# A gated attention and lookup-table FFN kernel: new orders in each group of 512 tokens, and one ScalarE copy for both halves of a looked-up block

## The reference

```python
xn = layernorm(x)                                  # x: 8 x 1024 x 512, fp32, rows of 512
q, k_i, v_i = xn @ Wq, xn @ Wk[i], xn @ Wv[i]      # 3 heads i, 128 wide
gate = softmax(xn @ Wg)                            # 3 numbers for a token
w_i = sigmoid(decay_logits[i]) ** max(s - t - 1, 0) where s > t, else 0   # diff = s - t
blended = sum_i gate_i * ((q @ k_i.T) * w_i) @ v_i
s = blended @ Wo * out_scale
G, U, Dn = lut[gate_idx], lut[up_idx], lut[down_idx]   # 16-entry table; 1376 x 512, 1376 x 512, 512 x 1376
h = silu(xn @ G.T) * (xn @ U.T)
y = x + s * silu(h @ Dn.T)
```

## Time and profile before

| | |
|---|---|
| three executions | 1935.11, 1935.36, 1942.34 us, median 1935.36 |
| profiled execution, its own time | 1939.05 us |
| its span | 1937.2 us |
| setup / 16 groups | 0 to 139.7 / 139.7 to 1937 us |
| mean granted TensorE clock | 0.987 |
| TensorE (PE) busy | 1826.7 us, 94% |
| VectorE (DVE), GpSimd (POOL), ScalarE (ACT) busy | 66%, 53%, 41% |

### The profile page before, as it was taken

The page is one execution under the profiler, slowest core; times in us unless marked ns, Lnnn a source line. Parts: engine busy times, 40 slices in busy tenths (PEclk is TensorE's granted clock), DMA queues, the critical chain, the costliest instruction groups (busy, mean ns, idle before and its releaser), DMA issues. The chain is left out here.

```text
span 1937.2 us, 45221 instructions
## 1 busy us (share of the span) xinstructions
PE 1826.7 (94%) x15944; PEld 1421.2 (73%) x15944; DVE 1287.3 (66%) x2629; ACT 803.3 (41%) x1445; POOL 1025.4 (53%) x1041
## 2 busy tenths in 40 slices
PE   6899999999999999899999999999999999999997
PEld 2337878687886878688776878768786887878786
DVE  7867657475865857476674758657574866748574
ACT  3773444343443343343443434333443434444342
POOL 9204728274562827447281745628283573828353
PEclk9999999999999999999999999999999999999999
DMA  9966666758675675757666686856767676676653
GB/s 227 350 241 165 176 183 164 191 162 225 157 184 165 172 199 159 212 154 186 184 164 176 162 221 157 195 159 172 198 160 204 157 195 183 161 195 164 184 152 106
DMA packets 401850, 354.53 MB, mean 183 GB/s; under 512 B 221553, under 2 KB 277617, under 8 KB 401537
## 3 DMA queue, kind: packets, MB, share of 16 engines
q1 hardware_dynamic: 390608, 344.57, 65.7%
q0 software_dynamic: 11008, 6.89, 2.4%
HBM read 277.56 MB, written 35.52 MB: 162 GB/s over the span
## 5 line engine op out<-in xcount | busy, mean ns | idle before, releaser
L1846 PE MATMUL F<-xtc,ring 128*128 128x256 f16 (+1 forms) x4224 | 501.2, 273 | 1.5 <-DVE region L1498 1.5
L1846 PEld LDWEIGHTS F<-xtc,ring 128*128 128x128 f16 (+1 forms) x4224 | 416.5, 100 | 45.9 <-DVE region L1498 3.5
L1846 PE MATMUL F<-xt,ring 128*128 128x256 f16 (+1 forms) x3168 | 385.8, 273 | 47.6 <-DVE region L1486 47.6
L1885 PE MATMUL F<-ring,region 128*128 128x256 f16 x3360 | 392.2, 277 | 0.0
L1846 PEld LDWEIGHTS F<-xt,ring 128*128 128x128 f16 (+1 forms) x3168 | 307.2, 100 | 92.7 <-DVE region L1486 60.0
L1885 PEld LDWEIGHTS F<-ring,region 128*128 128x128 f16 x3360 | 333.4, 99 | 52.9
L823 POOL TENSOR_TENSOR region<-hs,region 128x1024 f16<-128x1024 f32 x80 | 175.4, 2193 | 63.2 <-ACT region L909 63.2
L839 POOL TENSOR_TENSOR x_sb<-x_sb,region 128x512 f32<-128x512 f32 x64 | 81.0, 1265 | 192.0 <-DVE region L1585 192.0
L1731 PE MATMUL B<-xt,a_hi 128*128 128x512 f16 x512 | 158.4, 392 | 22.2 <-issue 17.5
L785 POOL TENSOR_TENSOR rstd<-var,nhalf 128x4 f32<-128x4 f32 x15 | 15.3, 1019 | 280.2 <-DVE var L1174 280.2
L909 ACT ACTIVATE region<-region 128x256 f16<-128x256 f32 x192 | 94.4, 500 | 166.5 <-DVE region L1518 166.5
(11 more groups left out here) (272 smaller groups left out, 3466.3 us busy)
## 6 DMA issues: line engine op xcount, KB each, us to landing
ring<-blocks SPq DMA_DIRECT2D x546, 256.0 KB, 3.1
ring<-dblocks SPq DMA_DIRECT2D x224, 256.0 KB, 3.1
x_sb<-in_x SPq DMA_DIRECT2D x64, 256.0 KB, 3.3
out_y<-x_sb SPq DMA_DIRECT2D x64, 256.0 KB, 3.5
ring<-blocks SPq DMA_DIRECT2D x112, 128.0 KB, 2.5
ring<-dblocks SPq DMA_DIRECT2D x112, 128.0 KB, 2.7
blocks<-ring SPq DMA_DIRECT2D x35, 256.0 KB, 8.0
x_sb<-codes SPq DMA_DIRECT2D x10, 512.0 KB, 9.2
```

What stands on the lines that cost most here:

```text
L1846: ins = T_.matmul(out_, a, b, start=fresh, stop=False, skip_group_check=True)
L1885: ins = T_.matmul(bank[:, j * HV:(j + 1) * HV], a, b, start=fresh, stop=False, skip_group_check=True)
```

## The change

The setup's two copies of a unit (high, low) become one over two neighbouring PSUM banks; `wd_hi` and `wd_lo` become one tensor. In the groups: the x work of tiles 0 and 1 moves to the values and the first set; the last set gets buffers of its own for YC and ZC (YB, ZB), so that its u4 need not wait for h2 of set 4, and that h2 moves behind c22 of set 5; `h_sums_high` of a set moves behind the first_copy two sets on; low2 of set 5 goes ahead on GpSimd; scores, retrieve and others shift; a copy of one column (`warm`) opens ScalarE's group 0 of an iteration; and TensorE does the next group's queries and keys ahead of the loop's end. `vb32` moves out of `xp`.

```diff
-            n += 4
+            n += 2
...
-        SCORES = {2: 0, 12: 1, 24: 2, 34: 3}
-        RETRIEVE = {6: 0, 17: 1, 29: 2}
-        PROBS = {3: 0, 13: 1, 25: 2}
-        LOWPR = {4: 0, 14: 1, 26: 2}
-        MIX = {11: 0, 18: 1}
+        SCORES = {3: 0, 12: 1, 24: 2, 34: 3}
+        RETRIEVE = {7: 0, 17: 1, 29: 2}
+        PROBS = {4: 0, 13: 1, 25: 2}
+        LOWPR = {5: 0, 14: 1, 26: 2}
+        MIX = {11: 0, 20: 1}
         UPDATE = {9: 0, 18: 1, 30: 2}
-        ROWS1 = {16: 0, 36: 1}
-        ROWS2 = {17: 0, 38: 1}
-        BLEND = {20: 0, 41: 1}
+        ROWS1 = {16: 0, 27: 1}
+        ROWS2 = {17: 0, 27: 1}
+        BLEND = {20: 0, 30: 1}
-        XHAT = {10: 0, 12: 1}
-        XLOW = {11: 0, 13: 1}
-        XPOSE = {15: 0, 17: 1}
-        XSUM = {16: 0}
-        XSUMHI = {20: 0}
-        XSUMLO = {22: 0}
+        XHAT = {1: 0, 3: 1}
+        XPOSE = {8: 0, 10: 1}
+        XSUMHI = {3: 0}
+        XSUMLO = {5: 0}
...
+        YB = [YC] * ND + [XC[ND % 2][:, 1:2]]
+        ZB = [ZC] * ND + [SC[ND % 2][:, 1:2]]
-        vb32 = xp[:, 0, 0:HD]
+        vb32 = at["bl"][:, 0:HD]
...
@@ GpSimd, a group @@
+                if not last:
+                    x_low(0)
+                    x_low(1)
+                    x_sums(0)
                 for n in range(NPG):
...
+                low2(ND)
                 h_sums_low(ND - 1)
                 low1(ND)
-                low2(ND)
@@ ScalarE, store in the setup @@
-                        copy(held(s, op, 0), LUHI[b % 2][:, n * w:n * w + w]).then_inc(s_wst, 1)
-                        copy(held(s, op, 1), LULO[b % 2][:, n * w:n * w + w]).then_inc(s_wst, 1)
+                        copy(held(s, op, slice(0, 2)), LU[b % 2][:, :, n * w:n * w + w]).then_inc(s_wst, 1)
@@ ScalarE, a group @@
+                if g == 0:
+                    copy(warm[:, :], dlog[:, 0:1])
...
                     copy(vb_hi[:, t], vb32[:, :]).then_inc(s_vbh, 1)
+                    if t in XHAT and not last:
+                        act.wait_ge(s_dwr[ND - 1], 16)
+                        x_high(XHAT[t], gi * GT + GT + XHAT[t] + 1)
...
                     if p == 0:
                         first_copy(s)
+                        if s >= 2:
+                            h_sums_high(s - 2)
                         if s:
                             high1(s - 1)
-                    if p == 1 and s:
+                    if p == 1 and 0 < s < ND:
                         high2(s - 1)
                     if p == 4:
                         silu1(s)
+                        if s == ND:
+                            high2(s - 1)
                     if p == 5:
                         silu2(s)
-                        if s:
+                        if s == ND:
                             h_sums_high(s - 1)
@@ VectorE, the values of a group @@
                     V_.tensor_tensor(vb_lo[:, t], vb32[:, :], vb_hi[:, t], ALU.subtract).then_inc(s_vbl, 1)
+                    if t in XHAT and not last:
+                        if XHAT[t] == 0:
+                            dve.wait_ge(s_tt, (gi * 2 + 2) * NTT)
+                            dve.wait_ge(s_xlo, gi * GT + GT)
+                        xhat_tile(1 - g, gi + 1, XHAT[t])
@@ VectorE, the sets @@
                 def u4(s):
-                    if s:
-                        dve.wait_ge(s_h2, q)
-                    else:
-                        dve.wait_ge(s_yr, gi * GT + FREE)
+                    if s == 0:
+                        dve.wait_ge(s_yr, gi * GT + FREE)
+                    elif s < ND:
+                        dve.wait_ge(s_h2, q)
...
                     if p == 1:
                         u2(s)
-                        if s:
+                        if 0 < s < ND:
                             h2(s - 1)
...
                     if p == 3:
                         c22(s)
+                        if s == ND:
+                            h2(s - 1)
@@ TensorE @@
+            queries_keys(0, 0)
             with pe.Fori(0, NB - 1) as i:
-                for g in range(GPB):
-                    group(i, g, False)
-            for g in range(GPB):
-                group(NB - 1, g, g == GPB - 1)
+                group(i, 0)
+                queries_keys(i, 1)
+                group(i, 1)
+                queries_keys(i + 1, 0)
+            group(NB - 1, 0)
+            queries_keys(NB - 1, 1)
+            group(NB - 1, 1)
```

More of the change, by code:

```diff
@@ L251, in attention_ffn_kernel @@
         oscale = sb("oscale", [P, 1], F32)
+        warm = sb("warm", [P, 1], F32)
         fade_q = sb("fade_q", [P, NH], F32)
@@ L351, in landed @@
             return 16 * (b // SLOTS + (b % SLOTS >= NDIR))
-        FB = [ps("F1"), ps("F2"), ps("F3"), ps("F4")]
+        fb = ctx.enter_context(nc.psum_tensor("F", [P, 4, BANK], F32))
+        FB = [fb[:, n] for n in range(4)]
         B = [ps("B0"), ps("B1"), ps("B2"), ps("B3")]
-        LUHI = [FB[0], FB[1]]
-        LULO = [FB[2], FB[3]]
+        LUHI = [FB[0], FB[2]]
+        LULO = [FB[1], FB[3]]
+        LU = [fb[:, 0:2], fb[:, 2:4]]
         s_x = [sem("x_in0"), sem("x_in1")]
@@ L948, in store @@
                         v0 = HV if u[0] == "ends" else 0
[L949 to L952, removed]
+                        to = stage[half[0]][:, half[1]] if half else wd[:, :, v0:v0 + HV]
+                        copy(to, LU[b % 2][:, :, at0:at0 + HV]).then_inc(s_wst, 1)
                 else:
@@ L1095, in group @@
                         high_probs(PROBS[n])
-                    if n in XHAT and not last:
-                        act.wait_ge(s_dwr[ND - 1], 16)
-                        x_high(XHAT[n], gi * GT + GT + XHAT[n] + 1)
                     if n in XSUMHI and not last:
@@ L1480, in u4 @@
                     dve.wait_ge(s_u2, q + 1)
-                    if s:
+                    if s == 0:
+                        dve.wait_ge(s_yr, gi * GT + FREE)
+                    elif s < ND:
                         dve.wait_ge(s_h2, q)
-                    else:
-                        dve.wait_ge(s_yr, gi * GT + FREE)
                     dve.wait_ge(s_pp, gi * NPG + s * NP + 3)
-                    V_.tensor_tensor(YC[0:M, 0:w], pair(3, s), XC[s % 2][0:M, 0:w], ALU.add).then_inc(s_u4, 1)
+                    V_.tensor_tensor(YB[s][0:M, 0:w], pair(3, s), XC[s % 2][0:M, 0:w], ALU.add).then_inc(s_u4, 1)
                 def c22(s):
@@ L1491, in c22 @@
                     dve.wait_ge(s_pp, gi * NPG + s * NP + 4)
-                    V_.tensor_tensor(ZC[0:M, 0:w], pair(2, s), YC[0:M, 0:w], ALU.add).then_inc(s_c22, 1)
+                    if s == ND:
+                        dve.wait_ge(s_hl2, q - 1 + 2 * FREE)
+                    V_.tensor_tensor(ZB[s][0:M, 0:w], pair(2, s), YB[s][0:M, 0:w], ALU.add).then_inc(s_c22, 1)
                 def c12(s):
@@ L1517, in h2 @@
                     dve.wait_ge(s_sg2, q + 1)
-                    V_.scalar_tensor_tensor(out=SC[s % 2][0:M, 0:w], in0=YC[0:M, 0:w], scalar=f_hf[0:M, 0:1],
-                                            in1=ZC[0:M, 0:w], op0=ALU.mult, op1=ALU.mult).then_inc(s_h2, 1)
+                    V_.scalar_tensor_tensor(out=SC[s % 2][0:M, 0:w], in0=YB[s][0:M, 0:w], scalar=f_hf[0:M, 0:1],
+                                            in1=ZB[s][0:M, 0:w], op0=ALU.mult, op1=ALU.mult).then_inc(s_h2, 1)
                 for n in range(NPG):
@@ L1549, in group @@
                         low_probs(gi, LOWPR[n])
-                    if n in XHAT and not last:
-                        j = XHAT[n]
-                        if j == 0:
-                            dve.wait_ge(s_vbl, gi * GT + GT)
-                        xhat_tile(1 - g, gi + 1, j)
                 c21(ND)
@@ L1779, in retrieve, with queries_keys @@
                 ins.then_inc(s_pu, 1)
-            def group(i, g, last):
+            def queries_keys(i, g):
                 gi = i * GPB + g
@@ L1795, in group @@
                                       xh[:, k], xl[:, k]) for k in range(KC)], GRP).then_inc(s_pqk, 1)
+            def group(i, g):
+                gi = i * GPB + g
+                xh, xl = xt_hi[:, g], xt_lo[:, g]
                 for t in range(GT):
@@ L1863, in chunk @@
                         hh, hl = ht[0:M, 0, cols], ht[0:M, 1, cols]
-                        wh, wl = wd_hi[0:M, v * HV:(v + 1) * HV], wd_lo[0:M, v * HV:(v + 1) * HV]
+                        wh, wl = (wd[0:M, half, v * HV:(v + 1) * HV] for half in range(2))
                         for a, b in ((hh, wh), (hh, wl), (hl, wh)):
```

13 lines of the change are left out of this document (5 added, 8 removed).

## The result

The changed kernel took 1969.24 us (median of four runs, 1967.95 to 1970.46), the kernel before beside it 1937.1. The ratio is 1.0162, interval 1.0138 to 1.0185: **slower by 1.6%**, where 1932 us and a range of 1880 to 1955 were forecast. The profiled execution took 1968.46 us, its span is 1966.6.

The account below looks back on a forecast made before the run. TensorE was taken as the bound, busy 1826.7 of 1937.2 us, leaving waits and low clock to win. Gains and costs summed to -3.4 us: 1935.6 from the profiled execution, 1932 from the runs' median; range 1880 to 1955.

Parts of the forecast that it names:

- Set 5: Product 5 of the last set: u4 no longer waits for h2, 2.25 us in each of 16 groups, -36.0 us.
- the half clock: TensorE at 1.2 GHz behind waits: -12 us behind u4's waits in set 5, +11.2 behind set 0's new idle stretch.
- sets 3 and 4: Waits for u4 there, caused by x work squeezed into GpSimd's sets 1 to 3, go: -21.7 us.
- -21.7: Gain in us from moving the x work out of sets 1 to 3, where GpSimd made u4 late.
- E11: TensorE's work ahead of the chunk at a group's end: its last third waits 0.2 us for GpSimd's low2(4).
- The values and set 0: Moved x work delays ScalarE: TensorE waits at product 4 and for silu1, +60.5 us, low clock behind it +11.2.
- Rival A: Set 0's second wait, for silu1, is absent because sums and copy finish in time: 1883 us; chance 0.25.
- The loop's end: TensorE's branch covered by longer matmuls and table load drawn ahead; VectorE's x-load delay priced at 0.8 us: -18.4 us.
- Setup: 92 ScalarE copies become 46 longer ones: between -3 and +1 us, taken as -1.
- The tail: Group's end: GpSimd makes E11 0.2 us late and the chunk wait 0.85 us where it waited 0.3: +14 us.
- Rival B: GpSimd bounds the end of set 5, its 7.2 us chain stretched by a fifth: +22, 1954 us; chance 0.15.

Follow-up runs that it names:

- f1: Changed kernel with the x work back at the kernel before's places beside sets 1 to 3; 1941.8 us, ratio 1.0055.
- e1: Changed kernel with ScalarE's copy of the first x sums behind silu2 of set 0 instead of ahead of silu1; 1930.9 us, ratio 0.9958.
- e3: Changed kernel with GpSimd's h_sums_low(4) made to wait until VectorE's low_probs(3) has ended; 1963.0 us, ratio 1.0122.
- e2: Changed kernel with ScalarE's h_sums_high(4) behind high1(5), high2(5) and high_probs(3) instead of ahead; 1936.5 us, ratio 0.9995.
- f4: Changed kernel with x sums copy behind silu2, h_sums_high(4) behind high_probs(3), SyncE's last blend transpose at piece 10 instead of 13; 1886.6 us, ratio 0.9773.
- e4: Kernel before with only queries and keys put ahead of TensorE's loop end, and ScalarE's warm copy; 1927.0 us, ratio 0.9944.
- f2: Kernel before with only set 5's own Y and Z blocks, u4 without its wait, h2(4) and high2(4) later; 1956.3 us, ratio 1.0123.

## Why the prediction was wrong, point by point

- **Set 5, the half clock, sets 3 and 4: right**, 67.0 us gained for 69.7 forecast. But "-21.7" is the price of the x work there only together with the old h sums: with the new ones (f1) the same places lose 48 us, 37 in sets 3 to 5 and 11 more at E11.
- **The values and set 0: right in the mechanism of the waits, a little large in size**: 53.0 of waits for 60.5. Rival A, at 0.25, did not come: every link took what its row said. By e1 this one place in ScalarE's queue cost 2% of the kernel. The half clock, 7.8 for 11.2, came near by luck: of five low stretches in the trace only two stand behind the wait for silu1 that the term was for, three behind waits of 2.9 to 3.7 us at scores 0 that the forecast did not have. In e3's trace 9 of the 15 waits for silu1 have one.
- **The loop's end: right in size (-15.2 for -18.4), wrong in place.** The gap at TensorE closed more than I thought; VectorE's lateness behind each loop end, with its standing at the x load, which I priced at 0.8 us, cost about 1.9 (11.5 / 6; single groups 0.2 to 3.9), at scores 0.
- **Setup: right.**
- **The tail is the step that failed.** It reads: "What is late next is GpSimd ... The chunk waits 0.85 us where it waited 0.3". The chunk's 0.86 and E11's place came as written (E11 about 0.5 us, not 0.2: low2(4), counted at 1.15 us, took 1.34, and h_sums_low(3) began 0.15 us later than counted). But the step stopped at the chunk. ScalarE's fourth instruction in that same queue, high_probs(3), was not followed: TensorE needs it, through low_probs(3), 1.3 us behind the chunk's start. It came 3 us after its input, then low_probs took 2.8 us beside GpSimd, and rows and blends behind it were late as well: 19.7 + 13.4 us unforecast, and with E11 and the chunk 37.6 too little in this one term. All other terms summed were 4 us off, the largest of them, the values and set 0, by 11. e2 gives the queue's share (1.6%); e3 shows by low_probs' durations that running side by side stretched it, with a share of the time too small to be told from noise; f4's trace shows what was left for SyncE's queue.
- **Rival B** named GpSimd at this place and 1954 us, but by a GpSimd chain stretched by a fifth. From h_sums_low(3) to the end of h_sums2(4) GpSimd took 7.5 us where 7.2 were counted; it was what waits in other engines' queues behind it that paid.

The low_probs could have been read beforehand: the trace of before had one of 2.38 us among 64 with a median of 0.83:
```profile
L1425 DVE TENSOR_TENSOR region<-faded,region x64: 551/826/2379, 167.4 to 1902.9; 128x384 f16<-128x384 f32 x64
```

## What to carry to other kernels

Where a wait on the bounding engine goes, follow every instruction it needs until its next wait with room to spare, through each engine's queue, and not only the first late one. An instruction that waits for a slow engine belongs behind all that are ready: three such moves (x_sums_high, h_sums_high(4), x_high(1)) and one transpose moved in SyncE's queue turned +1.6% into -3.5%. Price a VectorE operation with both inputs in SBUF by its longest duration where a long GpSimd operation can fall beside it. One profile's half clock is a sample, not a price: 21 executions of the kernel before, run beside e1 to e4, were granted 0.982 to 0.993 and took 1947.7 to 1927.1 us.

## What the runs showed of the hardware

- **VectorE beside GpSimd.** low_probs, two inputs in SBUF: 0.55 us alone, 2.80 beside low2(5) and h_sums_low(4), until 0.43 us after the latter's end, and 0.71 in e3 beside low2(5) alone. h2 has two inputs there as well; its mean over both shapes went from 1252 to 1765 ns:
```profile
L1518 DVE SCALAR_TENSOR_TENSOR region<-region,scale_hf 128x512 f32<-128x512 f32 x96 | 120.2, 1252 | 0.6
L1529 DVE SCALAR_TENSOR_TENSOR region<-region,scale_hf 128x512 f32<-128x512 f32 x96 | 169.4, 1765 | 0.6
```
Of the 80 at full width, 63 had an h_sums_low beside them before and 62 after, so it is not that they meet more often: they meet for longer. Beside h_sums_low and h_sums1 an h2 took 1.45 us in the mean before and 1.97 after. With no GpSimd instruction beside it, it took 0.75 in both (16 of them before, 3 after). The 16 of the last set took 0.48 alone before, and 1.26 beside low2(4) and h_sums2(4) after. VectorE's operations with one input in PSUM (u2, u4, c22, c12, c21) took 0.67 to 0.69 us in the mean with or without GpSimd beside them.
The Trainium skill ("SBUF — State Buffer", section "Who interferes with whom") says that a VectorE instruction with two inputs in SBUF contends with a GpSimd instruction that reads SBUF, that the port pair which they share is an exclusive lock, and that the order of issue decides who blocks. These rows agree. As I read the 2.80 us, they show besides that two GpSimd operations in a row are not parted: low_probs began 0.37 us into low2(5), and was let in only after h_sums_low(4). By that rule low_probs at the tail would have been priced at up to 2.1 + 0.7 us more, an estimate from the durations of those two.
- **The loop's end is paid on each engine.** Before, TensorE's branch took 4.0 to 4.5 us, and 16 matmuls of 256 columns started while it ran; in the changed kernel it took 3.4 to 4.4 us, and 16 or 17 matmuls of 512 columns did. With TensorE's covered, VectorE's idle time of 3.03 us there, and x landing late, were next: e4 kept 11 of the 32.6 us.
- **Half clock follows the waits.** f2 has 20 us of it behind waits of 2.75 us. f1, with no wait over 1.6 us in its groups, has no low stretch in them but the one of the last 8 us of the kernel, which every run has. How many of the waits near 2.5 us are followed by one differs from trace to trace (silu1: 2 of 15 in the changed kernel, 9 of 15 in e3).
